# Query and key stacks of a hybrid attention/SSM block: six transfers of 4 KB runs at one position in place of twelve of 1 KB runs at three

## What is computed

```python
H = 16; hd = D // H                       # 16 heads of 16 features
xn = x * rsqrt(mean(x * x) + EPS) * norm_w     # x already layer-normalised
q = (xn @ Wq.T + bq).reshape(B, T, H, hd).transpose(0, 2, 1, 3)
k = (xn @ Wk.T + bk).reshape(B, T, H, hd).transpose(0, 2, 1, 3)
v = (xn @ Wv.T + bv).reshape(B, T, H, hd).transpose(0, 2, 1, 3)
scores = einsum('bhqd,bhkd->bhqk', q, k) / sqrt(hd)    # causal mask
out = einsum('bhqk,bhkd->bhqd', softmax(scores), v)
out = out.transpose(0, 2, 1, 3).reshape(B, T, D) @ Wo.T + bo
return xn + out
```

## Time and profile before

| | us |
|---|---|
| median of 3 runs | 2177.48 |
| lowest, highest | 2174.78, 2177.67 |
| the profiled execution | 2174.6 |
| its span (first to last instruction) | 2172.8 |

### The profile page before, as it was taken

How to read it: one execution, slowest core, us unless ns; L and a number is a source line. 1 busy time by engine, 2 the same in 40 slices (tenths; PEclk the granted TensorE clock), 3 DMA queues, 4 the chain that set the end, 5 groups by cost and what they waited for, 6 DMA issues and landing times.

```text
span 2172.8 us, 33597 instructions
## 1 busy us (share of the span) xinstructions
PE 1840.5 (85%) x11393; PEld 1129.0 (52%) x11424; DVE 1675.5 (77%) x2570; ACT 1407.8 (65%) x2724; POOL 1087.5 (50%) x946
## 2 busy tenths in 40 slices
PE   5779788988889898988989888998989898868765
PEld 3446454646556464646556464655556464535333
DVE  5343678889788888879787888879887888977673
ACT  2445767686676767686775867687775777664531
POOL 0000365555455464656465454656555564666672
PEclk8999999999999999999999999999999999989887
DMA  4312377666767576666767576667767577651110
GB/s 114 83 53 58 92 156 152 150 138 142 144 149 159 128 168 146 154 136 146 164 133 154 136 157 137 149 138 157 161 136 155 124 161 145 132 113 45 41 57 10
DMA packets 185916, 275.53 MB, mean 127 GB/s; under 512 B 33537, under 2 KB 125586, under 8 KB 185746
## 3 DMA queue, kind: packets, MB, share of 16 engines
q1 hardware_dynamic: 155506, 163.27, 30.4%
q0 software_dynamic: 30240, 110.11, 27.3%
HBM read 128.58 MB, written 34.08 MB: 75 GB/s over the span
## 4 chain that ended last, share of the span: by engine, by line
PE 42%; ACT 19%; DMA 16%; SPq 7%; issue 5%; DVE 5%; POOL 5%; POOLq 0%; ACTq 0%; DVEq 0%
PE bank L312 7%; DMA sk<-qk_parts 6%; PE bank L516 5%; SPq L712 5%; PE bank L321 4%; ACT dec L896 3%; PE bank L370 3%; PE bank L393 3%; ACT pt L781 3%; PE bank L418 3%; DMA out<-X 3%; PE bank L499 3%; DMA qk_parts<-parts 3%; PE bank L480 2%; DMA y<-hc 2%
## 5 line engine op out<-in xcount | busy, mean ns | idle before, releaser
L1133 DVE TENSOR_TENSOR_SCAN hc<-dec,inp 128x1024 f32<-128x1024 f32 x256 | 613.2, 2395 | 42.5 <-ACT dec L896 30.5
L1304 POOL TENSOR_TENSOR inp<-u,b_all 128x512 f32<-128x512 f32 x256 | 355.3, 1388 | 393.7 <-DVE hc L1133 140.1
L781 ACT ACTIVATE pt<-bank 128x512 f32<-128x512 f32 x640 | 373.8, 597 | 223.8 <-PE bank L395 221.0
L1306 POOL TENSOR_TENSOR inp<-u,b_all 128x512 f32<-128x512 f32 x256 | 375.6, 1467 | 20.1
L370 PE MATMUL bank<-sk,sq 96*128 96x512 bf16 (+3 forms) x1024 | 278.5, 311 | 100.8 <-DMA sk<-qk_parts 64.9
L896 ACT ACTIVATE dec<-dt,a_neg 128x511 f32<-128x511 f32 x512 | 338.0, 717 | 32.6 <-DVE hc L1133 32.6
L1140 DVE TENSOR_TENSOR hc<-hc,bank 128x1024 f32<-128x1024 f32 x242 | 293.9, 1214 | 56.2 <-PE bank L555 55.3
L1313 POOL DMA_DIRECT2D y<-hc x210 | 186.1, 886 | 245.5 <-DMA y<-hc 121.5
L393 PE MATMUL bank<-sq,sk 98*128 98x512 bf16 (+3 forms) x1024 | 274.7, 307 | 35.7 <-ACT pt L781 30.0
L1012 DVE TENSOR_REDUCE mall<-bank 128x1 f32<-128x512 f32 x256 | 172.7, 675 | 108.2 <-PE bank L372 108.0
L370 PEld LDWEIGHTS bank<-sk,sq 96*128 96x128 bf16 x1024 | 102.0, 100 | 219.5 <-DMA sk<-qk_parts 74.0
(11 more groups left out here) (165 smaller groups left out, 3509.9 us busy)
## 6 DMA issues: line engine op xcount, KB each, us to landing
y<-hc POOLq DMA_DIRECT2D x210, 512.0 KB, 5.5
b_all<-b_kept SPq DMA_DIRECT2D x256, 256.0 KB, 4.0
qk_parts<-parts SPq DMA_DIRECT2D x96, 256.0 KB, 2.5
sq<-qk_parts SPq DMA_DIRECT2D x384, 64.0 KB, 3.7
sk<-qk_parts SPq DMA_DIRECT2D x384, 64.0 KB, 3.9
X<-in_x SPq DMA_DIRECT2D x16, 512.0 KB, 6.2
out<-X SPq DMA_DIRECT2D x16, 512.0 KB, 5.8
sq<-hlt SPq DMA_DIRECT2D x256, 2.0 KB
```

Of the source, the lines that this page charges most:

```text
L781: A(pt[:, n % PT, :], score_bank[unit % 2][:, :], ACT.Exp).then_inc(exp_done.sem, 1)
L1133: V.tensor_tensor_scan(h, d, v, 0.0, ALU.mult, ALU.add).then_inc(scan_done.sem, 1)
L1304: G.tensor_tensor(inp[:, n % 2, 0, :], u[:, 0, :], b_all[:, k % 3, :], ALU.mult).then_inc(pool_own.sem, 1)
L1306: G.tensor_tensor(inp[:, n % 2, 1, :], u[:, 1, :], b_all[:, k % 3, :], ALU.mult).then_inc(inp_ready.sem, 1)
```

## The change

The scratch tensor is laid out by half j first, then part. One transfer of 768 KB stores all three parts of a half (still in runs of 1 KB). The columns of the projection are reordered, (head, feature) to (feature, head), with the bias, so that in a part's 128 rows the four heads of one feature and group lie side by side: 4 KB in one run. For that the weights are first loaded into `xt_f`, which is free at that time, and the fold by the norm's weights writes them to `wqk` in the new order. The six pairs are reordered so that each part of the queries stands with a run of parts of the keys: part 0 with 0, 1, 2, part 1 with 0, 1, part 2 with 0. A stack is then six transfers: for each part of the queries one that repeats its 16 rows n times (n = 3, 2, 1) into `sq`, and one that takes n parts of the keys into `sk`. The source is written as n blocks of 16 rows, for `sq` with a step of 0 between blocks, and the destination as 16n partitions. All six are issued at p = 0. The bytes moved into `sq` and `sk` are the same: 768 KB a group.

```diff
-    TERMS = [(0, 0), (0, 1), (1, 0), (0, 2), (2, 0), (1, 1)]
+    TERMS = [(0, 0), (0, 1), (0, 2), (1, 0), (1, 1), (2, 0)]
-    NT = 2 * len(TERMS)
+    NT = 6
-        scratch = nc.dram_tensor("qk_parts", [NB, 3, C, 2, P, T], BF16, kind="Internal").ap()
+        scratch = nc.dram_tensor("qk_parts", [NB, C, 3, 2, P, T], BF16, kind="Internal").ap()
-        part_stored = tally("part_stored", 6, 16)
+        part_stored = tally("part_stored", 2, 16)
...
-                for part in range(3):
-                    sp.dma_start(scratch[a, part, j].rearrange("g p t -> p g t"),
-                                 parts[:, part, :, :]).then_inc(part_stored.sem, 16)
+                sp.dma_start(scratch[a, j].rearrange("q s p t -> p (q s) t"),
+                             parts[:, :, :, :].rearrange("p q s t -> p (q s) t")).then_inc(part_stored.sem, 16)
...
-            def stack(G, third):
+            def stack(G):
                 a, g = divmod(G, NG)
-                lo = (g % 2) * HG * HD
-                sp.wait_ge(part_stored.sem, part_stored.at(a, 3 * (g // 2 + 1)))
+                sp.wait_ge(part_stored.sem, part_stored.at(a, g // 2 + 1))
                 sp.wait_ge(st_ready.sem, st_ready.at(G - SLOTS))
                 sp.wait_ge(stacked.sem, stacked.at(G - 1))
-                for s in (2 * third, 2 * third + 1):
-                    jq, jk = TERMS[s]
-                    for dst, part, half_of in ((sq, jq, 0), (sk, jk, 1)):
-                        src = scratch[a, part, g // 2, half_of, lo:lo + HG * HD].rearrange("(h i) t -> i h t", i=HD)
-                        sp.dma_start(dst[s * HD:(s + 1) * HD, G % SLOTS, :, :], src).then_inc(stacked.sem, 16)
+                q_rows, k_rows = (scratch[a, g // 2, :, half_of].rearrange("q (i n h) t -> q n i (h t)", n=2, h=HG)[:, g % 2]
+                                  for half_of in range(2))
+                s = 0
+                for part in range(3):
+                    n = 3 - part
+                    for dst, rows in ((sq, q_rows[part:part + 1].to_broadcast([n, HD, HG * T])), (sk, k_rows[0:n])):
+                        sp.dma_start(dst[s * HD:(s + n) * HD, G % SLOTS, :, :].rearrange("k h t -> k (h t)"),
+                                     rows).then_inc(stacked.sem, 16)
+                    s += n
...
-                    if p < 3 and 0 <= q + 2 < NQ:
-                        stack(q + 2, p)
+                    if p == 0 and 0 <= q + 2 < NQ:
+                        stack(q + 2)
...
-                    act.wait_ge(part_stored.sem, part_stored.at(a, 3 * j))
+                    act.wait_ge(part_stored.sem, part_stored.at(a, j))
...
-                V.tensor_scalar(wqk[:, c, 0:D], wqk[:, c, 0:D], w_col[:, c:c + 1], HD ** -0.5, ALU.mult, ALU.mult)
-                last = V.tensor_scalar(wqk[:, c, D:], wqk[:, c, D:], w_col[:, c:c + 1], None, ALU.mult)
+                raw, folds = (t[:, c, :].rearrange(how, g=2 * C, i=HD)
+                              for t, how in ((xt_f, "p (g h i) -> p g h i"), (wqk, "p (g i h) -> p g h i")))
+                V.tensor_scalar(folds[:, 0:C], raw[:, 0:C], w_col[:, c:c + 1], HD ** -0.5, ALU.mult, ALU.mult)
+                last = V.tensor_scalar(folds[:, C:], raw[:, C:], w_col[:, c:c + 1], None, ALU.mult)
```

More of the change, by code:

```diff
@@ L672, in _ @@
             first = [
-                (wqk[:, :, :], chunked(wqk_t)), (w_col[:, 0:1], norm_w[0:P, None]), (w_col[:, 1:2], norm_w[P:, None]),
-                (bqk[:, :], bqk_c),
+                (xt_f[:, :, :], chunked(wqk_t)), (w_col[:, 0:1], norm_w[0:P, None]), (w_col[:, 1:2], norm_w[P:, None]),
+                (bqk[:, :], bqk_c.rearrange("(h i) c -> i h c", i=HD)),
             ]
```

## The result

| | us |
|---|---|
| median after | 2408.55 (2407.57 to 2411.62, 4 runs) |
| median before, same chip | 2176.13 (2173.36 to 2177.67, 4 runs) |
| ratio | 1.107, 95% interval 1.1043 to 1.1097 |
| span of the profiled execution | 2405.8, before 2172.8 |

The change makes the kernel 10.7% slower. The direction and the range of the prediction held. Its value, 2315, had the loss at 139 us; it is 232.

A forecast was written before the change was run, and what follows sets the result against it. PE, busy for 85% of the span, was taken to be held up in part by the path from parts to stack. 90 (steady batches) + 21 (start) + 28 (queued behind) = +139 on 2174.6, stated as 2315 us, range 2220 to 2430.

The forecast's parts named there:

- W: First issue of a stack to its last landing: 18 us in the steady part, 13.8 with nothing else running.
- Part 1 and 2: Single store of the parts: 0 us; fold and loads at the start: 0, at most 1 us either way.
- Part 3: SP's issuing of a stack: six issues take 3.3 us against 5.2 for twelve, saving 1.9 us a group.
- Part 4: DMA engines per stack transfer: four large on three or two, two small on sixteen; W 18 us, 15 to 23.
- Part 5: PE's delay from the late stack: +6.5 us a batch, +90 for fourteen batches, plus +21 at the start.
- The start: PE's delay in the first groups, where nothing covers the path: 27 x 0.8 = +21 us, between 10 and 30.
- Part 6: B's rows, output's store and L719's transfers queued behind the stack, and slow PE restart: 2 us a batch, +28.
- if POOL or DVE wait first, part 6 is: Sign in the profile after: if POOL or DVE wait first, Part 6 is wrong.
- The first rival: Stack transfers run on sixteen engines after all: W 7 to 8, PE's wait goes, -48 us, 2130; chance 0.13.
- It decides from W below 10.8: Condition in The first rival: it decides once W is below 10.8 us, the allowance of g = 2.
- The second rival: DMA engine 0 saturates, its work 35 us against a group's 30: about 2780 us; chance 0.10.

The follow-up runs named there:

- e1: Changed kernel with the two outer source dimensions of each stack transfer exchanged, so all six run on sixteen engines: 2182.97 us, ratio 1.0053.
- e8: Changed kernel with a stack's two largest transfers on sixteen engines and the next two left on two engines: 2231.17 us, ratio 1.0271.
- e9: Kernel before with scratch laid out by half and one 768 KB store for three, stack unchanged: 2168.34 us, ratio 0.9972.
- e4: Changed kernel with B's row of p = 0 issued between the parts' store and the stack: 2439.78 us, ratio 1.1209.
- e7: Changed kernel with B's row of p = 0 loaded at p = 8 of the q before: 2441.22 us, ratio 1.1246.
- e6: Kernel before with B's row of p = 0 loaded at p = 8 of the q before: 2161.17 us, ratio 0.9938.
- e5: e1 with B's row of p = 0 loaded at p = 8 of the q before: 2130.28 us, ratio 0.9801.
- e2: Kernel before with its twelve stack transfers of 1 KB runs all issued at p = 0: 2192.89 us, ratio 1.0097.
- e3: Changed kernel with twelve stack transfers of 16 partitions, 4 KB runs, in place of six: 2194.41 us, ratio 1.0079.

## Why the prediction was right, and where it was short

The mechanism was right: the narrow transfers make the change slow, and e1 and e8 show it. That the time fell into the range is in part luck. The range's upper end was reached through W = 20, and W was 15.8. With 15.8 in place of 18 the prediction's own sum is (5.0 - 1.3) x 0.85 x 14 = 44, and 44 + 21 + 28 makes some 2268: 140 us short, in the two terms named under parts 5 and 6.

**Part 1 and 2**, store and fold: right. e9 shows 0 to -0.5% for the store, and it lands in 3.7 us against the 4.0 worked out. The fold was not tried apart.

**Part 3**, SP's issues: a little low. The four large transfers take SP 0.74, 0.71, 0.63 and 0.62 us in the median, and a stack 4.0 us from the first issue to the end of the last, against 3.3. SP stands in the chain with 7% before and after.

**Part 4**, the engines: right to the packet, 108018. e1 settles the source's side of it. By the rule that the prediction named from the Trainium skill (page DMA: Bandwidth & Descriptors, section "Rules for kernel authors"), a leading broadcast of c copies, c under 16, confines a transfer to at most c engines; the trace agrees, with 42 completions a stack. The landing time was worked out well: at the start, W = 14.0 to 15.2 in the first seven groups against 13.8; an engine moved 25.6 GB/s, not 22.5, which makes 10.6 us for the 66 runs and leaves some 4 us of fixed time, not 1.8. (The 22.5 came from "337 to 362 GB/s"; the line in the earlier trace rows has 321 to 384, with nearly the same middle.) In the steady part g = 2 took 15.8 us in the median, not 18, most likely since POOL stood still in that window and sent little (e4, e7).

**Part 5**, PE's stall: right in kind. PE's wait for the stack rose by 118 us, where +7.6 us a batch and the start made 106 to 133. By groups it is g = 2: 7.2 us a batch of standing still, from 1.6; g = 1: 1.2, from 0; g = 0: 0.7, from 1.6. The start was under-sized. Its first seven stacks are 3.5 to 7 us late each, 37 us together where the sum had 27 x 0.8, and the loss up to the fourth load of X is 43.6 us. It goes with the engines: in e1, with the same positions and runs, that load is issued at 180.7 us, earlier than the 187.9 of the kernel before.

**Part 6** is the term that failed: "I add 2 us a batch for all this." A batch lost 14.2 us, of which PE's longer waits in g = 0 to 2 are some 6. The row of B lands 12.76 us after its issue, as worked out (8 to 10 us late), but the cover that I named for it, the 11 us until the scan, was not what ends first. POOL's list has the last norm's rsqrt, and it is behind the wait in the same queue. The trace of before had that row too: POOL's wait of 4.88 us in g = 2. e6 shows that even this one cost 0.6%. The prediction's own sign, "if POOL or DVE wait first, part 6 is" wrong, is what the profile shows.

Two more things in part 6 came out otherwise. X's load in g = 0 was to land near where it did; it is issued 21.8 us after the stack's first transfer in the median, 8.6 before, since the output's store ahead of it now takes 16.4 us to land and took 5.8. And POOL's y transfers stood in no term: they land in 6.2 us in the median where it was 5.5, and POOL's wait for them rose by 201 us. In e1 that wait is 149.0 us, so most of the rise goes with the narrow transfers. How a batch's 14.2 us divide among B's row, y and the clock (below) no run shows: e4 and e7, which moved the row, made PE's wait longer.

**The first rival**, sixteen engines, was given 2130 us. Its mechanism ran as e1 and gave 2183. PE's wait of 64.9 us did go but for 13.7, but the 48 us that it was to bring (0.8 of 64.9 is 52; the difference is small) did not come, because of the second path. e5, which clears both, gives 2130. The rival's step that failed is "It decides from W below 10.8": W was 8.6 in g = 2 and B's row decided. The second rival, saturation, did not come; at 25.6 GB/s a plain run of 4 KB takes 0.16 us, half of y's 0.31.

**A cost counted too low**: TensorE's clock. The prediction named the slow restart of an idle PE, as one of several things in the 2 us of part 6. In the stretch of 500 to 1700 us the granted clock is 0.98 before and 0.93 after. Unit 0 of G = 38 came after PE had stood still for 7.81 us and took 0.61 us, at a granted clock of 0.50, the lower of the two levels (1.2 GHz for 2.4); G = 36, without a stall, took 0.38. PE's busy time rose by 74 us for the same products, 4.6 a batch; how much of that lies on the path that ended last isn't shown.

## What to carry to other kernels

Before merging transfers, look at the outermost count on both sides: put the 16 or 128 rows outermost and the few blocks inside, and if the destination's row order has to change for that, change it on both operands of the product. Merged so, the stack was about as fast as twelve transfers (e1 1.0053, e2 and e3 1.0097 and 1.0079); with the blocks outermost it cost 10%. And a transfer that is slow for its own reader is slower still for whatever queues behind it: follow each load behind it to the next thing in its reader's list, not to the data's last consumer.

A wait that disappears from the profile is worth at most its length, and little if a second path ends just behind it. Here two ran side by side, and only the versions that cleared both were faster by 2%.

## What the runs showed of the hardware that was not expected

- The order of the source's dimensions alone, with the same destination, takes a transfer of 48 or 32 rows from sixteen engines to three or two: 108018 packets in the changed kernel against 111474 in e1.
- Two DMA engines moved 51 GB/s in 4 KB runs from DRAM to the SBUF over several microseconds with the other fourteen idle (changed kernel, 182 to 188 us, busy share 0.13), so one moved about 25.6, an estimate.
- 1 KB and 4 KB runs on sixteen engines made no difference to the time (e2 1.0097, e3 1.0079).
